# One 32-bit matmul per tile for the attended values, and seven of eight groups of h turned by 16-bit DMA transposes

## What is computed

```python
def xattn(hidden_states, decoder_hidden_states, Wq, Wkv):
    query = hidden_states @ Wq
    key, value = jnp.split(decoder_hidden_states @ Wkv, 2, axis=-1)
    scores = jnp.einsum('bqd,bkd->bqk', query, key) * scale
    return jnp.einsum('bqk,bkd->bqd', jax.nn.softmax(scores, axis=-1), value)

def ffn(x, w_gate, w_up, w_down):
    x = act_qdq(x)                                   # scale = max|x| / 32767
    up = act_qdq(x @ lpbq_dequant(w_up).T)
    gate = act_qdq(x @ lpbq_dequant(w_gate).T)
    gate = act_qdq(gate * fixed_qdq_u16(jax.nn.sigmoid(gate)))
    return act_qdq(gate * up) @ lpbq_dequant(w_down).T

x = x + xattn(layernorm(x), ctx_1024, Wq, Wkv)
x = x + ffn(layernorm(x), w_gate, w_up, w_down)
```

## Time and profile before

| | |
|---|---|
| runs | 913.06, 910.35, 917.38 us, median 913.06 |
| profiled execution | 914.32 us, span 912.5 us |
| busy | PE 877.3, DVE 658.1, ACT 567.7, POOL 145.8 us |
| granted clock of PE, mean | 0.991 |
| attention loop and scale of h | up to 138.06 us |
| gate product | 138.06 to 386.86 us |

### The profile page before, as it was taken

One profiled execution on the slowest core, in us unless ns is written; L12 is line 12 of the kernel. 1 busy time (PEld: TensorE's weight loads), 2 busy tenths in 40 slices (PEclk: granted clock), 3 DMA queues, 4 the chain that ended last, 5 costly groups with the idle time before them and its releaser, 6 DMA issues.

```text
span 912.5 us, 12151 instructions
## 1 busy us (share of the span) xinstructions
PE 877.3 (96%) x4308; PEld 442.6 (49%) x4308; DVE 658.1 (72%) x954; ACT 567.7 (62%) x693; POOL 145.8 (16%) x109
## 2 busy tenths in 40 slices
PE   7899979999999999999999989999599989999998
PEld 5788764444444444444444434444344434444443
DVE  4989896732436243279996859855899997999892
ACT  2369977634554354489997858853589975555330
POOL 0189950067001920000000000000000000000000
PEclk9999999999999999999999999999799999999999
DMA  9812226333459649884339994799987787989872
GB/s 342 326 71 117 93 94 242 155 156 138 162 220 294 222 155 294 319 314 162 138 144 334 358 339 145 276 364 354 409 293 264 270 325 273 389 300 394 305 278 106
DMA packets 92319, 226.57 MB, mean 248 GB/s; under 512 B 31984, under 2 KB 31984, under 8 KB 90096
## 3 DMA queue, kind: packets, MB, share of 16 engines
q1 hardware_dynamic: 91120, 221.80, 67.3%
q10 hardware_dynamic: 1152, 4.19, 1.2%
HBM read 127.40 MB, written 92.27 MB: 241 GB/s over the span
## 4 chain that ended last, share of the span: by engine, by line
PE 69%; issue 12%; DMA 8%; DVE 6%; ACT 3%; SPq 2%; POOLq 0%; POOL 0%; DVEq 0%; ACTq 0%
PE ps L837 27%; PE ps L870 16%; PE ps L915 14%; PE ps L942 3%; PE ps L710 3%; PE ps L771 2%; DMA big<-in_L_ffn_w_gate_dram 2%; PE ps L788 2%; DMA up_park<-big 2%; DMA big<-product_park 2%; DMA big<-sign_park 1%; DVE small L1463 1%; PE ps L932 1%; ACT big L960 1%; ACT big L1134 1%
## 5 line engine op out<-in xcount | busy, mean ns | idle before, releaser
L960 ACT ACTIVATE big<-ps 128x1024 f32<-128x1024 f32 (+2 forms) x194 | 153.8, 814 | 192.9 <-PE ps L837 104.5
L870 PE MATMUL ps<-big 128*128 (+1 forms) x1152 | 249.0, 379 | 2.5 <-ACT big L960 2.5
L837 PE MATMUL ps<-big 128*128 (+1 forms) x1152 | 248.8, 379 | 0.2 <-DVE big L1413 0.2
L870 PEld LDWEIGHTS ps<-big 128*128 128x128 f16 x1152 | 112.7, 98 | 138.7 <-issue 3.2
L837 PEld LDWEIGHTS ps<-big 128*128 128x128 f16 x1152 | 112.6, 98 | 136.1 <-DVE big L1413 0.8
L1431 DVE TENSOR_REDUCE small<-big 128x1 f32<-128x1024 f32 (+1 forms) x48 | 58.4, 1219 | 135.9 <-ACT big L960 135.8
L915 PE MATMUL ps<-big 128*128 128x512 f16 x576 | 126.7, 383 | 2.4 <-DVE big L1564 2.4
L915 PEld LDWEIGHTS ps<-big 128*128 128x128 f16 x576 | 56.7, 99 | 71.8 <-issue 5.1
L651 POOL PARTITION_ALL_REDUCE small<-small x9 | 3.6, 404 | 533.5 <-DVE small L1510 181.4
L896 PE MATMUL ps<-big 128*128 128x512 f16 x384 | 85.6, 385 | 3.4 <-ACT big L1167 3.4
L1481 DVE CUSTOM_DVE_ANT_0 big<-big,small 128x1024 f32<-128x1024 int16 x48 | 61.7, 1285 | 7.0 <-DVE small L1475 0.2
(11 more groups left out here) (103 smaller groups left out, 1008.9 us busy)
## 6 DMA issues: line engine op xcount, KB each, us to landing
big<-up_park SPq DMA_DIRECT2D x90, 512.0 KB, 5.7
up_park<-big SPq DMA_DIRECT2D x48, 512.0 KB, 4.8
gate_park<-big SPq DMA_DIRECT2D x42, 512.0 KB, 2.6
big<-gate_park SPq DMA_DIRECT2D x42, 512.0 KB, 6.1
sign_park<-big SPq DMA_DIRECT2D x48, 256.0 KB, 2.2
big<-in_x_dram SPq DMA_DIRECT2D x8, 1024.0 KB, 18.1
x_park<-big SPq DMA_DIRECT2D x8, 1024.0 KB, 3.9
product_park<-big SPq DMA_DIRECT2D x16, 512.0 KB, 6.0
```

Source lines behind the costliest of these rows:

```text
L837: mm = nc.tensor.matmul(ps[:, 2 * (n % 2) + j], w[:, a, k, o:o + P], XT[:, g, b, k], start=(k == 0 and a + b == 0), stop=(k == KC - 1 and ...
L870: mm = nc.tensor.matmul(ps[:, b + j], WU[:, a, k, o:o + P], XT[:, g, c, k], start=(k == 0 and a + c == 0), stop=(k == KC - 1 and c == 1))
L960: return nc.scalar.activation(dst, src, ACT.Copy)
```

## The change

The attended values come from one 32-bit matmul per tile: P and V stay whole, so `p_lo`, the common scale of V (`vmx`, `vs`, one `all_max`), its split and the multiplication of 1/sum by `vs` go. h is no longer turned on PE except in group 0: POOL writes all of h, unturned, into its final place `H` (before into a ring of four tiles), `h_max` reads it there, two tiles at a time but for the last two, and waits for POOL (`h2_d`) instead of for ACT. In the gate product ACT rounds a group of unturned h, SP turns it by four DMA transposes of four 128x128 blocks each (`turn_group`) into `hx`, and DVE splits what has landed there. Splits come one unit later than before and the last stands behind `gate_max(0)`.

```diff
+            def turn_group(g):
+                sp.wait_ge(hq_d, KC + g)
+                need(sp, hlo_d, KC + g - 2 if g > 2 else 0)
+                turned = hx[:, g % 2].rearrange("p (k i t) -> p k i t", k=KC, i=TI)
+                for i in range(TI):
+                    sp.dma_start(turned[:, :, i], hq[:, g % 2, i * D:(i + 1) * D],
+                                 transpose=True).then_inc((wd_turned, wu_turned)[g % 2], 16)
...
                     sp.dma_start(gate_d[g * UPG + n], gate_out[:, n % 2]).then_inc(g_st[n % 2], 16)
+                    if g == 0 and n + 2 < NG:
+                        turn_group(n + 2)
                     sp.wait_ge(sign_ev, g * UPG + n + 1)
...
+            turn_group(1)
             for g in range(4):
                 park_gate(g)
...
                 for i in range(TI):
-                    need(pool, ht_mm, TI * g + i - 3)
-                    nc.gpsimd.tensor_scalar(h2[:, i], X[:, g, i], negm[:, bass.ds(TI * g + i, 1)],
+                    nc.gpsimd.tensor_scalar(H[:, g, i], X[:, g, i], negm[:, bass.ds(TI * g + i, 1)],
                                             rs2[:, bass.ds(TI * g + i, 1)], ALU.add, ALU.mult).then_inc(h2_d, 1)
...
-                for a, b in ((0, 0), (0, 1), (1, 0)):
-                    mm = nc.tensor.matmul(ps[:, 5 + n % 2], PTs[:, n // TI % 2, a, n % TI], V[:, b, batch(n // TI)],
-                                          start=(a + b == 0), stop=(a == 1))
+                mm = nc.tensor.matmul(ps[:, 5 + n % 2], PTs[:, n // TI % 2, n % TI], V[:, batch(n // TI)],
+                                      start=True, stop=True)
...
-                if H_LAG <= n < NT + H_LAG:
+                if H_LAG <= n < TI + H_LAG:
                     turn_h(n - H_LAG)
...
             def h_int(g):
-                need(act, hlo_d, g + KC - 2 if g > 1 else 0)
-                nc.scalar.activation(hq[:, g % 2], HT[:, g].rearrange("p k t -> p (k t)"), ACT.Copy,
+                if g == 2:
+                    act.wait_ge(hlo_d, KC)
+                if g > 2:
+                    h_turned(act, g - 2)
+                nc.scalar.activation(hq[:, g % 2], H[:, g].rearrange("p i d -> p (i d)"), ACT.Copy,
...
             def h_max(n):
-                dve.wait_ge(ht_ev, n + 1)
+                lone = n + 2 >= NT
+                if not lone and n % 2 == 0:
+                    return
+                dve.wait_ge(h2_d, n + 1)
...
             def split_h(g):
                 hi, lo = (XT[:, g, l].rearrange("p k t -> p (k t)") for l in range(2))
-                dve.wait_ge(hq_d, g + KC)
-                nc.vector.tensor_copy(hi, hq[:, g % 2]).then_inc(hhi_d, 1)
+                h_turned(dve, g)
+                nc.vector.tensor_copy(hi, hx[:, g % 2]).then_inc(hhi_d, 1)
...
-                    if isinstance(g, int) and g == 0 and n + 2 < NG:
-                        split_h(n + 2)
+                    if isinstance(g, int) and g == 0:
+                        split_h(n + 1)
...
             gate_max(0)
+            split_h(NG - 1)
             linked(block_max(0, 1, wn_ld[1]))
```

More of the change, by code:

```diff
@@ L51 @@
 WTOP = 2048.0
+H_ODD = TI * (NG // 2)
+H_EVEN = TI * (NG // 2 - 1)
 KEPT = 23
@@ L165, in build @@
         HT0 = 16384
[L166 removed]
+        H = part(HT0, 16384).rearrange("p (g i d) -> p g i d", g=NG, i=TI)
         ctx_sb = part(HT0 + 4096, 1024).rearrange("p (b d) -> p b d", b=B)
         ctxT = part(HT0 + 5120, 1024).rearrange("p (k b s) -> p k b s", k=KC, b=B)
[L169 removed]
         KT = part(HT0 + 6144, 1024).rearrange("p (k s) -> p k s", k=KC)
@@ L285, in build @@
                  "pw0 pw1 pw2 rpw xs xinv fg gt gsc grc ginv fu usc uinv ut urc st ssc sinv src su ot osc "
-                 "oinv orc oo fin vmx vall vg vs vinv okn fin1").split()
+                 "oinv orc oo fin okn fin1").split()
         col = {n: sc[:, k:k + 1] for k, n in enumerate(names)}
@@ L691, in _ @@
                     quant_weights(g + 3, NBLK // 8, 0)
-            all_max(2, "hmx", "hall")
-            all_max(3, "wmx1", "wall1")
+            all_max(1, "hmx", "hall")
+            all_max(2, "wmx1", "wall1")
             pool.wait_ge(w_blk, 2)
             quant_weights(0, NBLK, 8)
-            all_max(4, "wmx2", "wall2")
+            all_max(3, "wmx2", "wall2")
             pool.wait_ge(w_blk, 3)
             quant_weights(0, NBLK, 9)
[L701 to L704, removed]
+            all_max(4, "gmx", "gall")
+            all_max(5, "smx", "sall")
+            all_max(6, "umx", "uall")
+            all_max(7, "omx", "oall")
         @block.tensor
@@ L795, in turn_h @@
                 for k in range(KC):
-                    mm = turn(ps[:, 7, k * P:(k + 1) * P], h2[:, n % 4, k * P:(k + 1) * P])
+                    mm = turn(ps[:, 7, k * P:(k + 1) * P], H[:, 0, n, k * P:(k + 1) * P])
                 mm.then_inc(ht_mm, 1)
@@ L972, in _ @@
             act.wait_ge(pro_mm, 9)
-            copy(Vf[:, 0], ps[:, 4]).then_inc(pro_ev, 1)
+            copy(V[:, 0], ps[:, 4]).then_inc(pro_ev, 1)
             for m in range(2):
@@ L978, in _ @@
             act.wait_ge(pro_mm, 12)
-            copy(Vf[:, 1], ps[:, 5]).then_inc(pro_ev, 1)
+            copy(V[:, 1], ps[:, 5]).then_inc(pro_ev, 1)
             NT = NG * TI
@@ L998, in take_pT @@
                 need(act, av_mm, TI * (g - 1))
-                copy(PTs[:, g % 2, 0], ps[:, 4].rearrange("p (i t) -> p i t", i=TI)).then_inc(pt_ev, 1)
+                copy(PTs[:, g % 2], ps[:, 4].rearrange("p (i t) -> p i t", i=TI)).then_inc(pt_ev, 1)
             def spread(n):
@@ L1009, in take_hT @@
                 act.wait_ge(ht_mm, n + 1)
-                t = (n % TI) * P
-                copy(HT[:, n // TI, :, t:t + P], ps[:, 7].rearrange("p (k t) -> p k t", k=KC)).then_inc(ht_ev, 1)
+                t = n * P
+                copy(first_h[:, :, t:t + P], ps[:, 7].rearrange("p (k t) -> p k t", k=KC)).then_inc(ht_ev, 1)
             def weights_hi(c, bank):
@@ L1020, in natural_hi @@
                     if m == 2:
-                        act.wait_ge(wu_turned, 16 * 8)
+                        act.wait_ge(wu_turned, 16 * (2 * KC + H_ODD))
                     else:
@@ L1066, in take_gate @@
                     elif n == 0:
-                        act.wait_ge(wd_turned, 16 * 2 * KC)
+                        act.wait_ge(wd_turned, 16 * (2 * KC + H_EVEN))
                     if not kept and not (isinstance(g, int) and g == 0 and n < 2):
@@ L1361, in _ @@
                     residual(n - X2_LAG)
-                if n % TI == 3 and TI <= n < NT + TI:
-                    p_lo(n // TI - 1)
                 if n + 2 * TI < NT:
```

71 lines of the change are left out of this document (26 added, 45 removed).

## The result

The changed kernel takes 928.93 us (median of 4 runs, 927.22 to 930.17) against 914.34 us before (median of 4 runs, 910.35 to 917.38; a fourth run, 915.61 us, has joined the three that gave 913.06): ratio 1.0161, 95% interval 1.0138 to 1.0184. It is slower by 1.6%. The forecast was 913.0 us, no change, with a range of 905 to 922; the time lies 6.9 us above the upper end of the range. The profiled execution took 927.91 us, span 926.1; the span before was 912.5, so the two traces differ by 13.6 us, and they tell where.

What follows compares the result with a forecast made beforehand. PE held most of the chain; POOL would bound the loop after the change. The gate product starting 4.3 us earlier and a 4.3 us PE stall cancel: 914.3, less 1.3 for the median, gives 913.0 us, range 905 to 922.

Steps and rivals of the forecast that it cites:

- POOL becomes the bound of the loop: Attention loop: POOL stays at 10.33 us a group, 0.9 us over PE, and ends at 125.4 us instead of 129.46.
- The partition maximum held by POOL's configuration: Between loop and gate product: POOL's configuration change delays the maximum to 5.5 us after POOL's end, 0.2 better than before.
- The start gain of 4.3 us: Start of the gate product: 4.1 + 0.2 = 4.3 us earlier, with bounds of 2.6 to 8.3.
- The clock at the gate: First gate units: PE's idle time of about 3 us may lower the clock, costing 1 to 2 us inside slack.
- What the transposes cost: Gate product: 2.56 us a group of h at 209 GB/s, 4.5 of a unit's 5.18 us with stores; group 7 lands at 180.
- The high end, 3.3 us a group: Gate product: transpose cost a group if it follows SP's issue times; PE then stalls 9.6 us.
- rival 3: Gate product: a transpose is priced per instruction, not per byte; at 2.2 us each, 941 us; chance 0.11.
- The stall: Gate product: group 7's late landing delays DVE's maxima and ACT's copy of unit 8; PE stalls 4.3 us before unit 10.
- The copies don't hold PE: Gate product: copies out of PSUM still come before PE needs them; the tightest, unit 3's, at 162 against 164.
- The signs named beforehand: Gate product: transposes under 1 us, DMA share near 1, group 7 split about 42 us in, one PE gap of about 4.
- rival 1: Gate product: transposes are hidden at 412 GB/s, 1.3 us a group, PE losing 0 to 0.9; 909 us; chance 0.17.
- The last step, 1.3 us off for the median: Final sum: the median of runs lies 1.3 us below the profiled execution, so 914.3 becomes 913.0 us.

Runs made afterwards that it cites:

- the later block maxima: Changed kernel with DVE's block maxima and scales of the up weights placed behind the gate maxima of units 6 and 7: 920.77 us, ratio 1.0072.
- group 1 ahead of the load: The repaired kernel with the first group's transpose issued ahead of the load of the up weights: 910.63 us, ratio 0.9958 to the kernel before.
- the repaired kernel: Changed kernel with one DMA transpose a group and DVE's block maxima behind the maxima of units 6 and 7: 910.86 us, ratio 0.9965 to the kernel before.
- longer `keep_warm`: The repaired kernel with 27 instead of 18 `keep_warm` matmuls ahead of the gate product: 910.02 us, ratio 0.9954 to the kernel before.

## Why the prediction was wrong

In one sentence: the term of the sum that failed is the cost of the transposes, 2.56 us a group taken by bytes from instructions of twelve blocks; as four instructions of four blocks each, a group holds SP for 5.45 us, and with its stores for 6.63 where 4.5 was forecast. The steps in their order:

**POOL becomes the bound of the loop: right.** 10.36 us a group, no waits, end at 124.5 (forecast 125.4, bounds 124.4 to 126.9). The start came 0.7 us earlier and all three later waits were gone; of the 2.45 us that could come back at the start, where 1.5 was taken, all came. That is the whole gain: a group took POOL 10.33 us before, so the loop's pace did not change, and the 0.7 us a group that the forecast takes off PE are not in the time. DVE's load was put too low: 8.8 us a group forecast, 37.20 us in four groups measured, 9.3; it still left POOL alone. The attend costs 0.87 us, forecast 0.90. The condition for another 1.7 us at the start, that the clock keeps its level, came true: it is 1.00 at 46 us.

**The partition maximum held by POOL's configuration: as forecast.** It ran 5.8 us after POOL's end (forecast 5.5), and 1.1 us after DVE had released it, so DVE is not what held it. In all variants that turn h by DMA it is 5.8 to 6.1. That the configuration holds it is argued from this steady distance; no run takes the change of configuration away. For the first call of freshly loaded code the Trainium skill (GPSIMD Engine Reference, 2.1 Instruction dispatch) gives about 6 us; this trace has 5.5 from the configuration's change. The start gain of 4.3 us was 4.9.

**The clock at the gate: right in kind.** Named as 1 to 2 us hidden in slack; it was 1.8 us. The slack it was to sit in was used up too, so it counts in full, and a second stretch at half clock behind the gap (2.1 us) was not in the sum. In the profiles of the kernels that turn h by DMA the idle time ahead of the gate product and the clock go together: with 1.1 to 1.8 us of it (one transpose a group, the later block maxima, both, and group 1 ahead of the load) the first units ran at 1.00, with 2.0 to 3.0 us (six kernels, the changed one among them) they lost 1.7 to 1.8 us. The clock a little earlier does not tell them apart: it was 0.54 from 120 to 125 us in the changed kernel and 0.50 from 124 to 128 in the repaired one. These are single executions, and no kernel changes the idle time alone from one side to the other. With the longer `keep_warm` there is no idle time and the clock is 1.00; but that run was no faster, since the repaired kernel had not lost its clock.

**What the transposes cost: wrong, and this decided it.** This is the step that failed. It took 2.56 us a group "by bytes", from 209 GB/s of full DMA engines. That row belongs to instructions of 12 blocks; a third of that size costs 1.27 us each, 5.45 a group, and leaves the engines at 0.42. A unit with its stores needs 6.63 us of SP and not 4.5, more than PE's 5.18, so SP never catches up. The high end, 3.3 us a group from SP's issue, scaled the 12-block times down with the blocks and so assumed away what it should bound. It was rival 3, "a price per instruction, not per byte", that came true, past its threshold of 3.8 us a group; its own price of 2.2 us each was the wrong size, so its 941 us was too dark. The argument against it, that the engines were full, only shows that at 12 blocks the price per instruction does not show. With one instruction a group the step holds nearly: 4.5 us forecast for a unit with its stores, 4.99 measured. Its sums have two slips that change nothing: 0.52 MB at 209 GB/s is 2.51 us, and a landing at 176.8 leaves a stall of 1.1 us, not 0.9.

**The stall: the mechanism right, its size from the wrong landing.** Forecast from the split of group 7 to the end of unit 8's copy: 14.2 us; measured 187.19 to 201.46, 14.3. Group 7 was forecast for 180 in the old frame; it was split 12.1 us later (187.19 + 4.87). 4.3 + 12.1 = 16.4, against waits of 14.3 and the slow first units of 1.8. The kernel with one transpose a group obeys the same rule: split at 178.77, its gate product 3.6 us early, so 2.4 us late in the old frame, and 4.3 + 2.4 is its gap of 6.7.

**The copies don't hold PE: wrong**, as one consequence: "the tightest is unit 3's" was worked out at 4.5 us a unit. At 6.6 ACT's rounding waited 4.45 us and PE 1.49 behind it, ahead of unit 7; ahead of unit 9 PE waited 1.05 us behind stores that were late on SP. The signs named beforehand say the same: issues of 1.27 us where under 1 was expected, a DMA share of 0.76 for near 1, group 7 split 54.0 us after the first gate matmul for 42, and a gap of 11.8 us for 4.

**The transposes at the rate of plain DMAs (rival 1): not in any kernel here**, though the repaired one hides them behind PE all the same. The page of the Trainium skill cited for it (Advanced Engine Details and Errata, X-Bar Transpose (TRN2)) expects 350 to 400 GB/s. The 16 blocks of a group are 0.52 MB, which makes 96 GB/s at 5.45 us, and at most 260 at the shortest 2.02 us. Another page of the Trainium skill (VectorE: DVE Perf Modes, The three transpose paths) gives 1309 ns for one 128x128 block by DMA. Here four blocks together take 1.27 us of SP and land in 2.5. Read as a price per instruction, that row gives an estimate of 5.2 us a group.

**The last step, 1.3 us off for the median**, rested on three runs; with the fourth the profiled execution stands at the median, and nothing had to be taken off.

Still open: what on SP or behind it takes the 1 us. The repaired kernel, 4.0 us ahead when the up product begins, ends only 1.6 us ahead in its profile; but that execution took 912.78 us, 1.9 us more than the kernel's median, and by the medians the kernel is 3.8 us ahead.

## What to carry to other kernels

A price per byte read from large DMAs can be far too low for small ones: where the engines were full, at 12 blocks, only bytes showed, and the price per instruction was hidden. Count the instructions, and join blocks until the queue and not the instruction sets the pace; here 28 transposes became 7 and gave back 9 us. When a step becomes a transfer, look for what stands behind its landing in each in-order list; block maxima that nobody waits for, 6.5 us and 10 with their scales, stood behind a late landing, and moving them away won 8.2 us, about as much as joining the transposes (8.8). And moving work off one engine wins nothing per group while another is as full: POOL took 10.33 us a group before and 10.36 after, and what was won at the start of the gate product were POOL's waits.

## What the hardware showed unasked

- A DMA transpose of four 128x128 16-bit blocks holds SP 1.26 to 1.27 us behind another transpose and 1.5 to 1.6 behind a store; one of sixteen blocks 2.02 us at the shortest and 3.5 us when the DMA engines are full.
- One transpose issued behind the load of 128x6144 32-bit weights (3.1 MB) holds SP 10.4 us, and every store queued on SP with it.
- The granted clock stood at half, the 1.2 GHz level, behind 11.8 us of idle time and cost 2.1 us more than the stall itself. The price did not follow the length: behind gaps of 6.7 and 4.3 us (one and two transposes a group) the 912 matmuls that followed lost 2.3 and 1.7 us.
